# A sequence layer with a routed mixture of experts: a scan with conjugate rotation, shared units woven into the GLU steps, blocks in pairs, landings counted by expert number

## The reference, cut to what matters

```python
def _L0_attn_ref(x, ...):                  # a state-space layer
    x_in = x @ in_W.T + in_b;  u = swapaxes(x_in, 1, 2)
    dtA = (-exp(log_A_real) + 1j * A_imag) * exp(log_dt)[:, None]
    k = 2 * einsum('hn,hnl->hl', Ceff, exp(dtA[:, :, None] * arange(Lseq))).real
    y = causal_convolution(u, k) + u * D_skip[:, None]          # by FFT in the reference
    y = gelu(y)
    a, g = split(glu_W @ y + glu_b[:, None]);  y = a * sigmoid(g)
    return y.T @ out_W.T + out_b + x

def _L0_ffn_ref(x, ...):                   # 14 routed experts (2 per token) and 2 shared ones
    gates = softmax(xf @ router_w);  top_v, top_i = top_k(gates, 2);  masked = normalised top_v
    routed = vmap(_ffn)(xf, rms_w, w1, w2)                      # silu(rmsnorm(x) * rw @ W1) @ W2
    return einsum('end,ne->nd', routed, masked) + shared.sum(0)

x = x + _L0_attn_ref(layernorm(x), ...)
x = x + _L0_ffn_ref(layernorm(x), ...)
```

## Time and profile before

| | us |
|---|---|
| median of 3 runs | 375.86 (373.63 to 376.33) |
| the profiled execution | 375.55 |
| its span, first to last instruction | 373.8 |
| busy: TensorE / its weight loads / VectorE / ScalarE / GpSimd | 265.4 / 242.9 / 229.7 / 186.1 / 187.6 |

### The profile page before, as it was taken

The page is one execution under the profiler, slowest core; times in us unless marked ns, Lnnn a source line. Parts: engine busy times, 40 slices in busy tenths (PEclk is TensorE's granted clock), DMA queues, the critical chain, the costliest instruction groups (busy, mean ns, idle before and its releaser), DMA issues.

```text
span 373.8 us, 9433 instructions
## 1 busy us (share of the span) xinstructions
PE 265.4 (71%) x2771; PEld 242.9 (65%) x2771; DVE 229.7 (61%) x922; ACT 186.1 (50%) x430; POOL 187.6 (50%) x236
## 2 busy tenths in 40 slices
PE   1694474743398485767645999799999999999500
PEld 0694364633385354554435899699999999999500
DVE  3979991499702575788675841166566566656455
ACT  0439364489954667666541233355544554555200
POOL 4686534000082001777777876077666665767500
PEclk9997588996579987888655799899999999999955
DMA  5790008888590000111111133333333233332199
GB/s 135 211 385 0 2 21 237 240 233 242 181 271 0 0 1 6 54 51 51 51 51 57 44 106 96 81 82 101 79 87 88 77 96 84 88 93 78 23 367 306
DMA packets 54574, 41.65 MB, mean 111 GB/s; under 512 B 6247, under 2 KB 50940, under 8 KB 54032
## 3 DMA queue, kind: packets, MB, share of 16 engines
q1 hardware_dynamic: 47552, 29.77, 28.3%
q0 software_dynamic: 4544, 8.47, 7.1%
q10 hardware_dynamic: 2448, 3.03, 2.5%
HBM read 29.14 MB, written 13.02 MB: 113 GB/s over the span
## 4 chain that ended last, share of the span: by engine, by line
PE 50%; DVE 18%; ACT 12%; issue 9%; DMA 4%; POOL 4%; ACTq 1%; DVEq 1%; POOLq 0%; SPq 0%
PE bank L1443 7%; PE bank L1451 6%; PE bank L1413 5%; PE bank L1406 5%; POOL y_dram L570 4%; ACT x_sb L1068 3%; PE bank L1354 3%; PE bank L1313 3%; PE bank L1221 2%; PE bank L1346 2%; DVE u L679 2%; PE bank L1256 2%; DMA rw<-in_L_ffn_router_w 2%; PE bank L1371 2%; PE bank L1436 2%
## 5 line engine op out<-in xcount | busy, mean ns | idle before, releaser
L570 POOL DMA_INDIRECT y_dram<-area,ybi x78 | 76.1, 976 | 45.1 <-issue 28.0
L564 POOL DMA_INDIRECT xs_dram<-area,pos x64 | 65.2, 1018 | 48.7 <-issue 48.4
L928 DVE COPY v<-v 128x512 f32 x83 | 37.8, 455 | 32.4 <-issue 32.2
L1443 PE MATMUL bank<-area,v 128*128 128x128 f32 x320 | 49.7, 280 | 0.0
L1451 PE MATMUL bank<-v,area 128*128 128x128 f32 x312 | 47.6, 275 | 0.0
L1174 ACT COPY area<-bank 128x128 f32<-128x128 f32 x81 | 21.6, 267 | 46.5 <-PE bank L1436 45.4
L1443 PEld LDWEIGHTS bank<-area,v 128*128 128x128 f32 x320 | 43.1, 196 | 0.0
L1451 PEld LDWEIGHTS bank<-v,area 128*128 128x128 f32 x312 | 41.1, 192 | 0.0
L1406 PE MATMUL bank<-v 128*128 (+1 forms) x256 | 36.8, 289 | 0.7 <-ACT area L1161 0.7
L1179 ACT ACTIVATE area<-bank 128x256 f32<-128x256 f32 x80 | 30.8, 385 | 12.5 <-PE bank L1443 12.3
L1413 PE MATMUL bank<-v,area 128*128 128x128 f32 x256 | 34.5, 279 | 0.2 <-DVE x_sb L898 0.2
(11 more groups left out here) (272 smaller groups left out, 561.0 us busy)
## 6 DMA issues: line engine op xcount, KB each, us to landing
area<-xs_dram SPq DMA_DIRECT2D x84, 65.0 KB, 1.9
area<-kp_dram SPq DMA_DIRECT2D x8, 512.0 KB, 6.4
x_sb<-in_L_attn_x SPq DMA_DIRECT2D x4, 512.0 KB, 8.8
area<-ab_dram SPq DMA_DIRECT2D x2, 1024.0 KB, 6.3
xn<-ab_dram SPq DMA_DIRECT2D x2, 1024.0 KB, 10.4
xn<-kp_dram SPq DMA_DIRECT2D x4, 512.0 KB, 6.5
v<-kp_dram SPq DMA_DIRECT2D x4, 512.0 KB, 7.2
area<-y_dram SPq DMA_DIRECT2D x4, 512.0 KB, 8.1
```

Of the source, the lines that this page charges most:

```text
L564: pool.indirect_dma_start(out=xs_dram.ap(), out_offset=bass.IndirectOffsetOnAxis(ap=pos[:, k, i:i + 1], axis=0), in_=hx[:, i, k, :], in_of ...
L570: pool.indirect_dma_start(out=y_dram.ap(), out_offset=bass.IndirectOffsetOnAxis(ap=ybi[:, z:z + 1].bitcast(U32), axis=0), in_=yb[:, z, :], ...
L928: v.tensor_copy(wc[:, z % STEP], v1_flat.rearrange("p (w m) -> p w m", w=2)[:, :, bass.ds(r, HID)]).then_inc(wc_ready, 1)
L1443: last = mm(bank[2 + z % 2][:, P * c:P * c + P], wc[:, z % STEP, 1, P * c:P * c + P], xsT[:, z % 3], start=True, stop=True)
```

## The change

- **Scan.** `weigh_states` now runs per group before the scan, straight from PSUM; the scan itself then rotates the weighed states with the conjugate factor, so nothing is weighed during or after it. `s_bd` is a buffer of its own, cleared by VectorE as its first instruction. Both table products are VectorE's. The norm's addition is spread: tiles 0 to 15 between ScalarE's evictions, 16 to 24 around the state copies, 25 to 31 on VectorE after its last copy. State copies take both batches at once. The turns of table 0 come before states 0, u's last three evictions after the first products, and the Hankel groups go to other buffers, each released earlier.
- **GLU steps.** CH + 1 steps. Routing lags by one chunk: x2 itself is turned (`turn_x2`), multiplied with a router matrix whose column means have been taken off, and scaled by the root at the logits. The semaphore pairs `done`/`need` become `drain`. From step 2 on a shared unit is woven in: `shared_in`, tanh on ScalarE, `gate_shared` on VectorE, `shared_out`, `add_group` (8 units in all); 10 more follow, evicted four at a time from one bank. The block tables are worked out on all partitions and turned to a row by two matmuls. Four of the 14 pads are issued by ScalarE.
- **Blocks in pairs.** Two blocks share each semaphore step, copy (L1174's), SiLU (L1179's) and result scaling; `yb` has 12 slots instead of 6. Two shared units run in the first part and two in each of the 6 iterations. The last six blocks are not in VectorE's loop.
- **The end.** A token's result goes to row `token` or `TOKENS + token` by whether its expert number is the lower or the higher of its two. `ltab` holds how many landings of each pair slot belong to blocks with work, for the first 13 experts and for all. SP waits for those counts, reads the low half in 4 pieces, then the high half in 8. TensorE adds x and the low half for the first four chunks into PSUM, VectorE does the other four; the high half is one more addition per chunk.

The diff, cut to its core:

```diff
-    SH_FIRST, SH_LOOP = 14, 3
+    SH_FIRST, SH_FILL, SH_LOOP = 18, 2, 2
+    WOVEN = 8
-        s_bd = area[:, 8192:12288].rearrange(...)
+        s_bd = sb("s_bd", [P, NPAIR, 2, NT])
-                for h_ in (xn_flat, area[:, 0:4096], area[:, 4096:8192], v1_flat[:, 4096:8192])]
+                for h_ in (area[:, 8192:12288], xn_flat, area[:, 0:4096], area[:, 4096:8192])]
...
-            for g in range(NG):
-                pool.wait_ge(mag_ready, g + 1)
-                pool.wait_ge(trig_ready, g + 1)
-                table_product(g_, g, 1).then_inc(v1_pool, 1)
...
+            def weigh_states(g):
+                dve.wait_ge(b_ps, g + 1)
+                ...
+                v.tensor_tensor(st[:, :, x_], lw[:, 1:3, x_]..., own, ALU.mult)
+                link(v.tensor_tensor(cross, lw[:, 5, x_]..., own[:, ::-1], ALU.mult))
+                v.tensor_tensor(st[:, :, x_], st[:, :, x_], cross, ALU.add).then_inc(st_dve, 1)
...
-            for i in range(CH + 2):
+            for i in range(CH + 1):
                 if i < CH:
                     glu(i)
-                chunk_step(i, i - 2)
+                chunk_step(i, i - 1, i - 3)
+                if 3 <= i < CH:
+                    add_group(i - 3, 1)
...
+            def gate_shared(u_):
+                dve.wait_ge(tanh_ready, u_ + 1)
+                z = half[u_ % 3].rearrange("p e m -> p (e m)")
+                v.scalar_tensor_tensor(out=z, in0=z, scalar=1.0, in1=bank[in_bank(u_)][:],
+                                       op0=ALU.add, op1=ALU.mult).then_inc(gated, 1)
...
+            def finish_pair(q, p):
+                row = z = 2 * p % UNROLL
+                dve.wait_ge(yb_ps, q + 4)
+                v.tensor_copy(ybi[:, z:z + 2].bitcast(U32), xs[:, row:row + 2, D].bitcast(U32))
+                v.tensor_tensor(yb[:, z:z + 2], bank[4 + p % 2][:, 0:2 * D]..., xs[:, row:row + 2, D + 1:D + 2]...,
+                                ALU.mult).then_inc(yb_ready, 2)
+                for j in range(2):
+                    fetch_weights(q * 2 + (STEP + j), z + j)
...
             with pe.Fori(0, LOOPS) as it:
+                for p in range(UNROLL // 2):
+                    g = STEP // 2 + p
+                    turn_rows(...g + 2); first_matrix(...g + 1); second_matrix(...g)
+                    if p % 3 == 0:
+                        shared_in_loop(it * SH_LOOP + (SH_BASE + p // 3))
+                    if p % 3 == 1:
+                        shared_out_loop(it * SH_LOOP + (SH_BASE + p // 3), p // 3)
...
-            for z in range(STEP):
-                sp.wait_ge(yb_out[z], 16 * (NBLK // STEP))
+            for z, r in enumerate(low):
+                sp.wait_ge(yb_out[z], r)
+            for c in range(CH // 2):
+                sp.dma_start(yl[:, 0, rows], y_tok[:, 0, rows]).then_inc(low_in[c], 16)
+            for z, r in enumerate(high):
+                sp.wait_ge(yb_out[z], r)
+            for c in range(CH):
+                sp.dma_start(yl[:, 1, rows], y_tok[:, 1, rows]).then_inc(high_in[c], 16)
```

More of the change, by code:

```diff
@@ L431, in _, with written @@
                 load_rows(z, z, 16 * 2 * NT if z == 0 else None)
-            with sp.Fori(0, LOOPS) as it:
+            def written(k, least):
+                _, counts = nc.values_load_multi_w_load_instructions(
+                    ltab[0:1, k], engines=[mybir.EngineType.SP], min_val=32 * (least // UNROLL), max_val=32 * (LOOPS + 1))
+                return counts
+            sp.wait_ge(ltab_ready, 1)
+            low, high = written(0, TOKENS // P), written(1, ROUTES // P)
+            with sp.Fori(0, LOOPS - 1) as it:
                 for z in range(0, UNROLL, 4):
@@ L722, in _ @@
+            for g in range(NG):
+                weigh_states(g)
+            dve.wait_ge(st_dve, NG)
             sv = st[:].rearrange("p r x (b j) -> p r x b j", b=B)
@@ L806, in chunk_step @@
                     v.tensor_tensor(lgm, lg, over_experts(best[:, :, 0]), ALU.subtract).then_inc(lg_ready, 1)
-                    need(a)
+                    for i in range(TILES):
+                        v.max_index(which[:, i, :], best[:, i, :], lg[:, i, :])
+                if norm:
+                    for i in range(TILES * c, TILES * c + TILES):
+                        v.bn_stats(stats[:, i, :], x_sb[:, i, :])
+                if unit >= 0:
+                    gate_shared(unit)
+                v.drain()
@@ L958, in _ @@
+            for p in range(STEP // 2):
+                finish_again((LOOPS - 1) * (UNROLL // 2) + STEP + p, p, 32 * LOOPS)
+            add_looped(NT - 1)
+            dve.wait_ge(so_added, NT)
+            for c in range(CH // 2, CH):
+                rows = slice(4 * c, 4 * c + 4)
+                if c % 2 == 0:
+                    dve.wait_ge(low_in[c // 2], 16)
+                last = v.tensor_tensor(x_sb[:, rows], x_sb[:, rows], yl[:, 0, rows], ALU.add)
+            link(last)
             for c in range(CH):
@@ L964, in _ @@
+                v.tensor_tensor(x_sb[:, rows], both, yl[:, 1, rows], ALU.add).then_inc(sum_ready, 1)
         @block.scalar
@@ new lines, in second_matrix @@
+            def second_matrix(q, p, kept=None):
+                pe.wait_ge(act_ready, q + 3)
+                if kept is not None:
+                    pe.wait_ge(yb_ready, kept)
+                for j in range(2):
+                    for c in range(HC):
+                        last = mm(bank[4 + p % 2][:, D * j:D * j + D], act_sb[:, p % 3, HID * j + P * c:HID * j + P * c + P],
+                                  wc[:, (2 * p + j) % STEP, 0, P * c:P * c + P], start=(c == 0), stop=(c == HC - 1))
@@ new lines, in _ @@
+            pe.wait_ge(xt_ready, NBLK // 2 + 4)
+            pe.wait_ge(act_ready, NBLK // 2 + 3)
+            pe.wait_ge(so_added, SH_BASE)
+            for c in range(CH // 2):
+                rows = slice(4 * c, 4 * c + 4)
+                if c % 2 == 0:
+                    pe.wait_ge(low_in[c // 2], 16)
+                mm(bank[c][:], ident[:], x_sb[:, rows].rearrange("p i d -> p (i d)"), start=True, stop=False)
+                mm(bank[c][:], ident[:], yl[:, 0, rows].rearrange("p i d -> p (i d)"), start=False, stop=True).then_inc(sum_ps, 1)
```

897 lines of the change are left out of this document (518 added, 379 removed).

## The result

The changed kernel takes 344.18 us (median of four runs, 339.24 to 347.99) where the kernel before takes 376.1 (373.63 to 377.72) in the same session. The ratio of 0.9068 (95% interval 0.8985 to 0.9152) is that of the fast runs alone, 340.74, 339.24 and a fifth of 342.6 us, and leaves out those of 347.62 and 347.99 us as slow ones. Forecast were 345.0 us and a range of 336 to 358. The profiled execution is the one of 347.62 us, span 345.9, at a mean granted clock of 0.888; the runs of 339 to 341 us had 0.92 to 0.93. Where that matters it is said.

The account below looks back on a forecast made before the run. No single engine bounds it: ScalarE's chain in the scan, GpSimd's scatters in the GLU steps, TensorE in the block loop. From 375.55 us, savings of 10.0, 4.6, 7.0 and 9.0 give about 345 us, range 336 to 358.

Parts of the forecast that it names:

- To the GLU steps, -10 forecast: Start to first turn of y: earlier Hankel loads and a shorter scan chain save 10 us (bounds 6 and 12.5).
- GLU steps to the first block, -4.6 forecast: First turn of y to first block: 22.5 us to the first scatter plus 92, saving 4.6 us.
- 10.2 us, level with GpSimd: GLU steps: a step with woven shared units takes 10.2 us, GpSimd's pace for one chunk's scatters; bounds 9.5 and 11.5.
- The rival of the starving steps: GLU steps: steps of 11.5 to 12 us starve the scatter, 9 to 13 us more, 354 to 358; chance 0.14.
- Drains at nothing: GLU steps: 14 drains a step in place of semaphore waits cost 0 us, bounds -0.5 and +2.4.
- The loop, -7.0 forecast: Block loop: 14 shared units instead of 18, 926 matmul instructions plus fill, 106.5 us, saving 7.0 us.
- stall of pairs: Block loop: waits of 0.5 us in each of 39 pairs, about 10 us with the end, 355; chance 0.12.
- falling clock: Block loop: waits in each pair lower TensorE's clock; 376 us at 0.77, 430 at 0.55; chance 0.03.
- slack shrinks: Block loop: 12 blocks take 15.6 us on TensorE, 15.3 on GpSimd; stalls of 0 to 3 us may come.
- The end, -9.0 forecast: Behind the block loop: overlapped loads and 12 additions instead of 16 give 14.0 us, saving 9.0 (bounds 5 and 11).
- some 7 us before TensorE ends: The end: the high half can be loaded once block 72 has landed, some 7 us before TensorE ends.
- GpSimd held by VectorE: Block loop: weight copies each hold a send for 0.455 us, 135 us instead of 103, 377 in all; chance 0.02.

Follow-up runs that it names:

- the one profiled again: The changed kernel run once more without any edit, for a second profile: 345.26 us, ratio 0.9152.
- with semaphores: Each drain of the changed kernel replaced by VectorE's wait on its own semaphore, raised by the instruction before: 337.25 us, ratio 0.9016.
- with units moved: Six shared units of the changed kernel moved from before the block loop into it: 351.67 us, ratio 0.9364.
- the run behind all landings: The changed kernel with both halves of y loaded only when every send has landed: 352.47 us, ratio 0.9422.
- the third group: Four runs on a third chip, where the kernel before takes 448.7 us and the unedited changed kernel 410.32 us.

## Why the prediction was right, and where it was not

**To the GLU steps, -10 forecast, -14.0 measured.** The order of events is as forecast: products of two in 2.4 us, the first Hankel issue early, a Hankel gap for a kernel not yet written. The sizes are better throughout. The issue is at 46.83, not 48.8 (which should have been 49.4, as 54.66 less the 5.3 us of the eviction), because u's eviction begins at 29.82 instead of 32.51 where I held "no earlier"; the three last groups end at 90.58, not the 93.4 that I worked out with the gap, and the scan (90.2 forecast) at 90.5. The choice of 92.5 between 90 and 93.4 was the error, 2 us. The other 2 us are a claim that the GELU stage "keeps its 15.7 us": it takes 13.6, its first 48 reads 3.06 us instead of the 5.34 of the earlier trace rows. Before, TensorE came to them from 6.00 us of idle time and was granted 0.51 from 102.5 to 107.8 us; now it comes from the Hankel matmuls and is granted 0.93 from 90.6 to 93.6.

**GLU steps to the first block, -4.6 forecast, -0.9 measured.** The first scatter comes 21.7 us after the first turn of y (22.5 forecast). From it to the first block it is 96.6 us, not 92; the term "10.2 us, level with GpSimd" failed in this execution and in the one profiled again (96.7). The rival of the starving steps came true in part, and with it a sign that the prediction had named as wrong, gaps between scatters. It goes with TensorE's clock: where the steps are granted 1.00 the same code takes 10.2 us a step and 90.2 from first scatter to first block (125.17 to 215.35), under the forecast, and at 0.65 to 0.80 up to 12.7. I had read the 0.79 and costed the woven units at it, but took TensorE's 3.83 us of idle time as room. They are no room where its products lie on the path from one glu to the next. Drains at nothing were wrong too: 0.046 us each, 0.65 a step, inside my bounds.

**The loop, -7.0 forecast, -7.8 measured.** Right in mechanism and size: TensorE is busy 104.86 of 105.4 us at clock 1.00; no stall of pairs, no falling clock. The sends run at 1.28 us back to back and fall behind by 4.3 us at the end, the "slack shrinks" of the forecast, felt only there.

**The end, -9.0 forecast, -5.2 measured.** 14.0 was 1.9 + 8.3 + 3.8; measured are 2.4 until VectorE adds, 9.5 for 12 additions with waits of 0.52 and 1.24, and 5.9 from the last one to the end, 17.8 in all. The step that failed is the landing: "some 7 us before TensorE ends" took 2.1 us of landing after a send in time. The send lagged, and its landing took 5.9 us beside the low half's loads. The last 2 us are the transfers: from 331.4 to 344.4 us the DMA engines are full with the high half and the outputs, which the prediction had named only as a bound ("the output's 2 MB may queue"). In four profiles of the first chip (the first, the one again, with semaphores, with units moved) the end comes 15.8, 16.0, 15.4 and 16.2 us after the issue of the high half's loads. So an issue that comes later moves the end by about as much, and faster additions alone would bring little; the latter is argued, not tried.

**The rivals.** GpSimd held by VectorE: not by 0.455 us a send. The sends' durations in ns, shortest, median, longest; then one of the longer ones with the second of the two copies beside it:

```profile
L610 POOL DMA_INDIRECT y_dram<-u x78: 967/974/1493, 227.3 to 332.4; - x78
298.02 1.20 POOL L610 DMA_INDIRECT y_dram<-u  x1 [0.30 <-issue]
298.79 0.67 DVE L990 COPY v<-v 128x512 f32 x1 [0.42 <-issue]
```

The median is that of the earlier trace rows with two weight copies in a row beside them. Nine more sends take 1.04 to 1.24 us, seven of them with both copies of a pair over them, and in four of these the second copy takes 0.67 to 0.69 us instead of 0.43. Together that is 1.3 us of sends. The two last, 1.35 and 1.49 us, lie beside VectorE's additions, and without those, in the run behind all landings, the last ones take 0.98 and 0.97. So the lock that the Trainium skill states (SBUF — State Buffer, SBUF: two separate sides) may show at the end with half a microsecond a send: the section has it for operations with two inputs in SBUF too, against a GpSimd operation that reads SBUF, and the first additions are such operations. In the loop it may show in those nine, and not at the rival's price in each of 78.

## What to carry to other kernels

Cost a chain through TensorE at both levels of its clock; idle time of an engine is room only for work beside the path, not for work in it. When two transfers are to overlap, ask what the earlier one does to the landing that the later one waits for: here 2 MB in front made it 5.9 us instead of 2.1. Where errors of both signs meet, read each term against its stretch before you call a sum right. An ordering device that is free in one place costs its difference times the number of times it stands on the path; count them before calling it nothing.

## What the runs showed of the hardware that I had not expected

- A drain spaces small linked operations 0.24 us apart, a semaphore on the same engine 0.20.
- With TensorE's idle time filled, its granted clock was lower (0.71 instead of 0.80), not higher.
- The same program differs by 20% between chips (374.33 and 447.95 us for the kernel before). In the unedited kernel of the third group everything up to the first scatter takes as long as on the first chip (124.53 and 123.98 us); from there a step is 14.4 us, and the block loop takes 138.9 us instead of 105.4. VectorE waits 1.9 to 4.3 us in each of six steps for something that the profile puts down to no engine of the core:

```profile
164.74 0.27 DVE L889 TENSOR_TENSOR u<-u,bank 128x112 f32<-128x112 f32 x1 [4.30 <-remote]
```

TensorE had ended the ranks that it waits for at 161.5 us. The 4.3 us are about the difference between 14.4 and 10.2; what they are stays open. Waits of the same kind, up to 6 us, stand on VectorE and ScalarE in the block loop.
